# Experts of a token-routed layer: from 96 tiles of 128 rows to 80 pairs of 64-row tiles on the two halves of TensorE's columns

## The reference

```
logits = x @ router_w                      # 2048 tokens, 32 experts
probs = softmax(logits);  topk_w, topk_idx = top_k(probs, 4);  topk_w /= sum(topk_w)
act = silu(x @ w_gate[e]) * (x @ w_up[e])  # 256 -> 192, for each of a token's 4 experts e
routed = sum over e of topk_w * (act @ w_down[e])      # 192 -> 256
shared = silu(x @ sh_gate) * (x @ sh_up) @ sh_down * sigmoid(x @ sh_gate_w)
x = x + tanh(g_ffn[1]) * (routed + shared)
```

## Time and profile before

| | us |
|---|---|
| time, median of 3 runs | 1495.78 |
| lowest and highest of them | 1491.2 and 1495.98 |
| time of the profiled execution | 1492.29 |
| its span, first to last instruction | 1490.6 |

### The profile page before, as it was taken

How to read it: one execution, slowest core, us unless ns; L and a number is a source line. 1 busy time by engine, 2 the same in 40 slices (tenths; PEclk the granted TensorE clock), 3 DMA queues, 4 the chain that set the end, 5 groups by cost and what they waited for, 6 DMA issues and landing times. The chain is left out here.

```text
span 1490.6 us, 24628 instructions
## 1 busy us (share of the span) xinstructions
PE 1290.0 (87%) x8472; PEld 995.4 (67%) x8472; DVE 749.2 (50%) x1642; ACT 673.0 (45%) x1507; POOL 649.1 (44%) x600
## 2 busy tenths in 40 slices
PE   2899862999999999999999199996969899999970
PEld 0555541888888888888888167775636666666640
DVE  2677635444444444455443256664565444444437
ACT  1677731545555455555453065563212155555530
POOL 3222104466666555566664222210112277777740
PEclk9999975999999999999999599997789999999995
DMA  5333343344444444445443465002000155555528
GB/s 156 43 58 58 54 131 130 76 105 106 104 104 106 102 99 99 99 99 103 117 88 36 119 193 190 23 2 71 30 1 1 56 162 159 161 159 162 147 72 282
DMA packets 173340, 151.33 MB, mean 102 GB/s; under 512 B 79414, under 2 KB 141884, under 8 KB 173249
## 3 DMA queue, kind: packets, MB, share of 16 engines
q1 hardware_dynamic: 137152, 93.52, 21.7%
q0 software_dynamic: 33792, 54.57, 18.2%
q10 hardware_dynamic: 2304, 2.10, 0.4%
HBM read 112.37 MB, written 41.94 MB: 104 GB/s over the span
## 5 line engine op out<-in xcount | busy, mean ns | idle before, releaser
L1084 POOL DMA_INDIRECT x_dram<-e_y,rows x128 | 218.4, 1706 | 198.7 <-ACT e_y L1188 174.0
L1117 PE MATMUL bank<-e_xg_hi,e_w_hi 128*128 128x512 f32 x512 | 158.4, 391 | 0.0
L1117 PE MATMUL bank<-e_xg_hi,e_w_lo 128*128 128x512 f32 x512 | 158.0, 390 | 0.0
L1076 POOL DMA_INDIRECT e_xtok<-xn_dram,rows x128 | 125.5, 981 | 74.5 <-issue 38.4
L1117 PE MATMUL bank<-e_xg_lo,e_w_hi 128*128 128x512 f32 x512 | 157.7, 389 | 0.0
L1178 ACT CAST e_hidden_hi<-e_hid 128x512 fp32r<-128x512 f32 x128 | 79.5, 621 | 160.1 <-DVE e_hid L1222 160.1
L1222 DVE TENSOR_TENSOR e_hid<-e_sg,bank 128x512 f32<-128x512 f32 x128 | 88.1, 688 | 125.0 <-PE bank L1117 91.0
L1683 PE MATMUL bank<-e_wt,e_xT 128*128 128x384 f32 x384 | 148.5, 510 | 0.7 <-ACT e_wt L1727 0.6
L1225 DVE TENSOR_TENSOR e_hidden_lo<-e_hid,e_hidden_hi 128x512 fp32r<-128x512 f32 x128 | 88.6, 692 | 88.0 <-ACT e_hidden_hi L1178 88.0
L1659 POOL DMA_INDIRECT ys_dram<-e_yt,tile_dest x96 | 97.0, 1011 | 54.5 <-issue 35.0
L1117 PEld LDWEIGHTS bank<-e_xg_hi,e_w_lo 128*128 128x128 f32 x512 | 96.4, 188 | 20.2
(11 more groups left out here) (264 smaller groups left out, 2547.2 us busy)
## 6 DMA issues: line engine op xcount, KB each, us to landing
e_w<-in_L_ffn_w SPq DMA_DIRECT2D x48, 512.0 KB, 5.0
e_wd<-in_L_down SPq DMA_DIRECT2D x96, 192.0 KB, 2.8
wgu<-in_L_gate_up SPq DMA_DIRECT2D x8, 1536.0 KB, 7.3
c_y<-ys_dram SPq DMA_DIRECT2D x16, 512.0 KB, 8.3
X<-in_x SPq DMA_DIRECT2D x1, 2048.0 KB
b_cT<-in_ctx_t SPq DMA_DIRECT2D x8, 256.0 KB, 6.1
v_dram<-b_vtok SPq DMA_DIRECT2D x16, 128.0 KB, 1.8
b_vs<-v_dram SPq DMA_DIRECT2D x16, 128.0 KB, 3.4
```

The source lines that it names most:

```text
L1076: nc.gpsimd.indirect_dma_start(out=xtok[q][:, :], out_offset=None, in_=xn_dram[:, :], in_offset=bass.IndirectOffsetOnAxis(ap=rows[:, e, q: ...
L1084: nc.gpsimd.indirect_dma_start(out=x_dram[:, :], out_offset=bass.IndirectOffsetOnAxis(ap=rows[:, e, q:q + 1], axis=0), in_=y[q][:, :], in_ ...
L1117: last = nc.tensor.matmul(bank[f % 2][:, :], w[:, k * F0 + f * 128:k * F0 + (f + 1) * 128], x[:, k, h * SLOTS:(h + 1) * SLOTS], start=(w, ...
```

## The change

The tiles become half as high (TT = 64) and are run in pairs (PT = 128 rows). `PAIRS` = 80 pairs replace the 96 tiles. The two tiles of a pair can have different experts. Gathers, scatters, transposes, Silu and the copies of VectorE and ScalarE stay as they were, one for each pair. `up` and `down` become two matmuls in place of each one, with 64 stationary columns each: tile u of the pair goes to half u of the array's columns and of the PSUM partitions, and has its own weights as moving operand. So two sets of weights are needed for a pair: ScalarE copies those of tile 0, VectorE those of tile 1 (new), SyncE loads two sets of down weights, with three buffers for each in place of four. Both `take_weights` now stand last in their loop and run one pair further ahead; in VectorE's loop `take_tokens` stands ahead of `gated`. The routing finds the number of tiles by an add and a shift in place of a comparison with all edges and a sum, and the experts of even and odd tiles in two columns. The diff, cut:

```diff
-TT = 128
+TT, PT = 64, 128
-TILES = -(-((B * S * TOPK + E1 * (TT - 1)) // TT) // 4) * 4
+PAIRS = -(-(B * S * TOPK + E1 * (TT - 1)) // PT)
...
-            count = upto[:, B, :].rearrange("p (e o) -> p e o", o=1).broadcast_to((128, E1, B * S // TT))
-            ch.link(nc.vector.tensor_tensor(over[:, :, :], count, edge[:, :, :], ALU.is_gt))
-            ch.link(nc.vector.tensor_reduce(ntiles[:, :], over[:, :, :], AX_X, ALU.add))
+            ch.link(nc.vector.tensor_scalar(whole[:, :], upto[:, B, :], float(TT - 1), None, ALU.add))
+            ch.link(nc.vector.tensor_scalar(tiled[:, :], whole[:, :], TT.bit_length() - 1, None, ALU.logical_shift_right))
+            ch.link(nc.vector.tensor_copy(ntiles[:, :], tiled[:, :]))
...
-            ch.link(nc.vector.tensor_scalar(done[:, :], ends[:, :], tile_at[:, 0:1], None, ALU.is_le))
-            ch.link(nc.vector.tensor_reduce(te[:, :], done[:, :], AX_X, ALU.add))
+            for u in range(2):
+                last = nc.vector.tensor_scalar(done[:, u, :], ends[:, :], tile_at[:, u:u + 1], None, ALU.is_le)
+            ch.link(last)
+            ch.link(nc.vector.tensor_reduce(te[:, :], done[:, :, :], AX_X, ALU.add))
...
-    NBUF = 4
+    NBUF = 3
...
             def load_down(t):
-                e = sp.value_load(tile_expert[0:1, t:t + 1], min_val=0, max_val=E1 - 1)
-                sp.dma_start(wd[t % NBUF][:, :, :].rearrange("p k n -> p (k n)"),
-                             a["L1_down"][bass.ds(e, 1), :, :].rearrange("o p n -> p (o n)")).then_inc(wd_in[t % NBUF], 16)
+                for u in range(2):
+                    e = sp.value_load(tile_expert[0:1, u, t:t + 1], min_val=0, max_val=E1 - 1)
+                    sp.dma_start(wd[t % NBUF][u][:, :, :].rearrange("p k n -> p (k n)"),
+                                 a["L1_down"][bass.ds(e, 1), :, :].rearrange("o p n -> p (o n)")).then_inc(wd_in[t % NBUF], 16)
...
                 for k in range(KD):
-                    last = nc.tensor.matmul(GU[t % 2][:, 0:2 * F1], xT[t % 2][:, k, :],
-                                            wt[t % NBUF][:, k * 2 * F1:(k + 1) * 2 * F1], start=k == 0, stop=k == KD - 1)
+                    for u in range(2):
+                        last = nc.tensor.matmul(GU[t % 2][half(u), 0:2 * F1], xT[t % 2][:, k, half(u)],
+                                                wt[t % NBUF][u][:, k * 2 * F1:(k + 1) * 2 * F1], start=k == 0, stop=k == KD - 1)
...
                 for m in range(2):
-                    last = nc.tensor.matmul(Y[t % 2][:, 0:D], hidT[t % 2][:, m, :], wd[t % NBUF][:, m, :],
-                                            start=m == 0, stop=m == 1)
+                    for u in range(2):
+                        last = nc.tensor.matmul(Y[t % 2][half(u), 0:D], hidT[t % 2][:, m, half(u)], wd[t % NBUF][u][:, m, :],
+                                                start=m == 0, stop=m == 1)
...
@@ scalar
             gate(0)
+            take_weights(NBUF)
             gate(1)
...
-                if t + NBUF < TILES:
-                    take_weights(t + NBUF)
-                if t + 1 < TILES:
+                if t + 1 < PAIRS:
                     take_hidden(t + 1)
+                if t + NBUF + 1 < PAIRS:
+                    take_weights(t + NBUF + 1)
@@ vector
+            def take_weights(t):
+                e = dve.value_load(tile_expert[0:1, 1, t:t + 1], min_val=0, max_val=E1 - 1)
+                if t >= NBUF:
+                    dve.wait_ge(gu_ps, t - NBUF + 1)
+                nc.vector.tensor_copy(wt[t % NBUF][1][:, :], wgu[:, bass.ds(e, 1), :].rearrange("p o n -> p (o n)")
+                                      ).then_inc(wt1_sb, 1)
...
             take_tokens(0)
             take_tokens(1)
+            for t in range(NBUF):
+                take_weights(t)
             gated(0)
             take_tokens(2)
+            take_weights(NBUF)
             gated(1)
-            for t in range(TILES):
-                if t + 2 < TILES:
+            for t in range(PAIRS):
+                if t + 3 < PAIRS:
+                    take_tokens(t + 3)
+                if t + 2 < PAIRS:
                     gated(t + 2)
-                if t + 3 < TILES:
-                    take_tokens(t + 3)
                 take_result(t)
+                if t + NBUF + 1 < PAIRS:
+                    take_weights(t + NBUF + 1)
```

More of the change, by code:

```diff
@@ L1308, in routing1_phase @@
         value = sb("value", [128, TOPK, B])
-        places = sb("places", [128, TT])
-        tiles = sb("tiles", [128, TILES])
+        places = sb("places", [128, PT])
+        tiles = sb("tiles", [128, PAIRS])
         at_place = [t[:, :, :].rearrange("p b e -> p (b e)").rearrange("p (k n) -> p k n", k=TOPK) for t in choice]
[L1312 to L1318, removed]
+        at_tile = [t[:, :, :].rearrange("p b e -> p (b e)")[:, 0:TOPK * PAIRS].rearrange("p (k n) -> p k n", k=TOPK)
+                   for t in (ex, mine, member, expert)]
+        found, empty = (t[:, :, :].rearrange("p b e -> p (b e)")[:, 0:PAIRS] for t in (before, totals))
+        clipped = sb("clipped", [128, PAIRS], I32)
+        tile_at = sb("tile_at", [128, 2])
+        done = sb("done", [128, 2, E1])
+        te = sb("te", [128, 2])
         (wr_in, w_in, xb_sb, xt_ps, xt0_sb, xt1_sb, l_ps, made, max_sb, ex_sb, sig_sb, mem_sb, cnt_ps, te_sb, te_ps,
@@ L1349, in _ @@
             iota(expert[:, :, :], [[0, B], [1, E1]])
[L1350 to L1353, removed]
+            iota(tile_at[:, :], [[1, 2]], 2)
+            iota(places[:, :], [[1, PT]])
+            iota(tiles[:, :], [[1, PAIRS]])
             iota(value[:, :, :], [[B * S, TOPK], [S, B]], 1, 1)
@@ L1430, in find @@
                 for k in range(TOPK):
-                    last = nc.tensor.matmul(MAP[:, 0:TILES], at_place[b % NMAP][:, k, :], at_tile[b % NMAP][:, k, :],
+                    last = nc.tensor.matmul(MAP[:, 0:PAIRS], at_place[b % NMAP][:, k, :], at_tile[b % NMAP][:, k, :],
                                             start=b == 0 and k == 0, stop=b == B - 1 and k == TOPK - 1)
@@ L1458, in _ @@
             pe.wait_ge(te_sb, 1)
-            nc.tensor.matmul(TE[0:1, 0:128], te[:, :], r.ident[:, :], start=True, stop=True).then_inc(te_ps, 1)
+            for u in range(2):
+                last = nc.tensor.matmul(TE[0:1, u * 128:(u + 1) * 128], te[:, u:u + 1], r.ident[:, :], start=True, stop=True)
+            last.then_inc(te_ps, 1)
             down(1)
@@ L1663, in _ @@
             for v in range(NXT):
-                pool.wait_ge(y_out[v], 16 * (TILES // NXT))
+                pool.wait_ge(y_out[v], 16 * len(range(v, PAIRS, NXT)))
         @block.tensor
@@ L1672, in turn_over @@
                 for k in range(KD):
-                    last = nc.tensor.transpose(XT[t % 2][:, k * TT:(k + 1) * TT], xt[t % NXT][:, k * 128:(k + 1) * 128],
+                    last = nc.tensor.transpose(XT[t % 2][:, k * PT:(k + 1) * PT], xt[t % NXT][:, k * 128:(k + 1) * 128],
                                                r.ident[:, :])
@@ L1691, in turn_hidden @@
                 for m in range(2):
-                    last = nc.tensor.transpose(HT[t % 2][0:FH, m * TT:(m + 1) * TT], hid[t % 2][:, m * FH:(m + 1) * FH],
+                    last = nc.tensor.transpose(HT[t % 2][0:FH, m * PT:(m + 1) * PT], hid[t % 2][:, m * FH:(m + 1) * FH],
                                                r.ident[:, :])
```

75 lines of the change are left out of this document (40 added, 35 removed).

## The result

The changed kernel takes 1462.32 us (median of 4 runs, 1458.5 to 1463.18), the kernel before 1495.3 beside it: ratio 0.9778, 95% interval 0.9759 to 0.9797. That is 33 us less; the forecast was 30.8 less than the 1495.8 known then, to 1465. The profiled execution took 1461.86 with a span of 1460.1, 30.5 under that of before; the sum had -29.5.

The account below looks back on a forecast made before the run. TensorE was taken to bound the experts' stage: 96 tiles at 2.72 us become 80 pairs at 2.89, -29.9, with -0.4 and +0.8 making -29.5. That gave 1462.8 or 1466.3; forecast 1465 us, range 1455 to 1484.

Parts of the forecast that it names:

- the sum: Whole kernel: -29.9 for the experts' stage, -0.4 for routing, +0.8 for the first `up`, together -29.5 us.
- The bound: Experts' stage: TensorE, busy 100 of 100 us there, stays the bound, with a period of 2.89 us per pair.
- Full overlap of the halves: `up` and `down`: half-width matmuls on different columns run side by side, so work stays 2.58 us, plus 0.03.
- The switch: TensorE, once in and out per pair: changing between full and divided array costs 0.28 us, bounds 0.18 to 0.35.
- The four terms: Array change per pair: 0.09 in, 0.04 first weight load, 0.09 out, 0.06 second transpose's load, in us.
- the later starts: `up` and `down` per pair: 0.03 us added because the second half's matmuls start later.
- The stalls: TensorE before `up`: 0.06 us waiting for `xT` and 0.075 of unhidden weight load per tile, both go.
- The new copy: VectorE's 128 x 768 weight copy between SBUF tensors takes 0.57 us per pair, hidden under TensorE.
- Routing and start: Routing chain -0.6 and a small matmul 0.2, net -0.4 us; first `up` +0.8 us, bound 1.5.
- The last pairs drain as before: End of the experts' stage: no change in time for the last pairs.
- The first rival: Experts' stage: GpSimd's DMAs and VectorE's new copy exclude each other, period 3.05 to 3.17, 1478 to 1487 us; chance 0.18.
- Its DMAs still at 1.0: Sign in the experts' stage: GpSimd's DMAs keep 1.0 us; the prediction is wrong if they grow.

Follow-up runs that it names:

- Experiment 4: Changed kernel with `turn_over(t + 3)` moved between `down` and `up`, so full-width transposes split the half-width work once more per pair: 1482.31 us, 0.992 of before.
- experiment 3: Changed kernel with loops of `up` and `down` exchanged, all of tile 0's matmuls before tile 1's: 1465.55 us, 0.9797 of the kernel before.
- experiment 5: Changed kernel with the halves one behind the other and, from the third pair, both tiles' outputs on columns 0 to 63: 1629.25 us, one run.
- the grouping: Changed kernel with two pairs' work between two changes of TensorE's array, plain copy: 1507.41 us, 0.9728 of before; repeated 1505.42 us, 0.9702.
- experiment 1: Kernel before, whole tiles of 128, with VectorE's `take_tokens` ahead of `gated`: 1482.75 us, 0.9911 of before.
- experiment 2: Changed kernel with `gated` back ahead of `take_tokens`: 1462.09 us, 0.9778 of the kernel before.
- the other form: Changed kernel with VectorE's weight copy written as the larger of each value and itself: 1506.89 us, 0.9734 of before; repeated 1507.79 us, 0.971.

## Why the prediction was right

*The bound.* It said that TensorE stays the bound. Experiment 4 shows it for the first chip: 0.30 us more work, 0.30 us more period.

*Full overlap of the halves.* Predicted 0.03 for tile 1 beside tile 0, from a burst of 32 columns. Shown by experiments 3 and 5, whose kernels differ in nothing but the columns: 1.51 against 2.75 for `up`. They ran on different chips, but the record of `up` takes 486 ns in both. The 0.03 wasn't there: the second half's record starts 0.007 behind the first's. What the trace of before couldn't tell, and what I then got wrong in the expectation of experiment 3, is whether the order in the program matters. It hardly does.

*The switch.* Predicted 0.28 (0.18 to 0.35), measured 0.30 by experiment 4, 2 x 0.145 = 0.29 by the grouping, and 0.284 between the periods of experiment 1 and of the kernel after (2.594 and 2.878). The four terms hold too, by the starts in the trace of after: into the half width 0.09 (predicted 0.09), the first load 0.05 (0.04), out 0.10 (0.09), the second transpose 0.04 (0.06). The short neighbour in attention was enough. The full-width work, put at 2.58, is the 2.594 of experiment 1; this 0.014 too little and the 0.03 too much for the later starts leave the 2.89 for 2.88.

*The stalls.* That both go was right, and experiment 1 shows that both had one cause. The text didn't say what this implies: without half tiles the same 0.12 a tile, 12 us, could be had by order alone. In the kernel after, the new order isn't what removes them (experiment 2); the later `down` does.

*The new copy.* 0.57 predicted, 0.56 measured: the slope of the like operations held from 256 to 768 elements. Three of the 80 copies took 0.60 to 0.78.

*Routing and start.* -0.4 predicted; the chain, from the first copy of the counts to the addition that TensorE waits for, fell from 15.77 to 15.16, by the 0.6 predicted. From there to the first transpose 0.86 came back, most of it before the list `tile_rows` was done, where the text had only a small matmul of 0.2. What took it wasn't looked into. The sum of this term was +0.25 and not -0.4. +0.8 was predicted for the first `up`, +1.1 measured, within its bound of 1.5. VectorE's two copies of tokens were done at 1181.53, and 0.60 more went before its first weight copy at 1182.13:

```profile
1180.74 0.79 DVE L1782 COPY e_xT<-bank 128x256 f32<-128x256 f32 x2 [4.31 <-PE bank L1681]
...
1182.13 0.56 DVE L1775 COPY e_wt<-wgu 128x768 f32 x1 [0.60 <-issue]
1182.76 0.32 PEld L1693 LDWEIGHTS bank<-e_wt,e_xT 128*64 128x64 f32 x4 [2.10 <-ACT e_wt L1738]
1182.79 1.55 PE L1693 MATMUL bank<-e_wt,e_xT 128*64 128x384 f32 x4 [1.73 <-DVE e_wt L1775]
```

That is the 0.60 where I had taken 0.2 for reading the register. The copy is what `up` waits for: with the other form, 0.40 longer, `up` starts 3.21 behind the first transpose instead of 2.81.

*The end.* "The last pairs drain as before" was wrong twice, with opposite signs. The last results are copied 1.37 and 1.36 us apart instead of 1.09 and 0.86, as each `turn_hidden` and `down` now costs a round trip of the array, and the last `down` waits 0.28 for its e_wd: +1.0. Then the first load of `combine` starts 6.89 us after the last scatter instead of 9.54: -2.6. All the other kernels with pairs have 6.88 or 6.89 there, and the other whole-tile kernel (experiment 1) has 9.54, so it belongs to the change and not to the execution. Its cause wasn't tried. That the sum of -29.5 came within 1 us of the 30.5 is partly luck: the +1.4 ahead of the chain and the -2.2 at the end (+1.0, -0.6, -2.6), which the text didn't have, nearly cancel.

*The first rival.* Its mechanism is real and its price was far off. Scatters beside the weight copy take up to 1.36 instead of 1.01, but their mean is only 0.09 above. All scatters and all copies from 1200 to 1400 us (least, median, most, in ns):

```profile
L1667 POOL DMA_INDIRECT ys_dram<-e_yt,tile_dest x69: 1012/1014/1361, 1201.2 to 1398.3; - x69
...
L1775 DVE COPY e_wt<-wgu x70: 559/560/783, 1201.0 to 1399.5; 128x768 f32 x70
```

With a scatter of 1.10, a gather of 1.01 and 0.30 of idle time behind each, GpSimd needs 2.71 for a pair, still 0.17 under TensorE. "Its DMAs still at 1.0" is the one mark of the prediction that failed, and the text had named it as a sign that the prediction is wrong; as such it was too strict. It cost nothing: a scatter and a copy that meet do so for only 0.24 us on average, and GpSimd has the 0.17 to give. What matters is which starts first. The 72 operations of GpSimd that start inside a copy take 1.13 in the mean; the 15 in which a copy starts keep their 0.99, and there the copy takes 0.58, at most 0.78. The rival's full blocking, up to 1.0 for VectorE and 0.57 for GpSimd, occurs nowhere. The Trainium skill, SBUF — State Buffer, section "SBUF: two separate sides", says that such a copy keeps GpSimd from writing descriptors, and that a VectorE operation with two SBUF inputs stands only against a GpSimd operation that reads SBUF. By the first half the trace agrees in kind. The operation with two inputs held the scatters longer than the copy did (1.40 against 1.10), and more than the 1.01 of those that it doesn't touch; whether a scatter counts there as a reader of SBUF, by its list of rows, no run here shows.

## What to carry to other kernels

When small groups leave a matmul's stationary side half filled, put two on different column halves: they run together, in whatever order the program has them, and the price is one round trip of the array, 0.29 us here, so do as much divided work as possible between two full-width operations. Before such a rebuild, read the present period for stalls and remove them alone: here an exchange of two calls had 12 of the 33 us. Compare on one chip: a stage that TensorE's work bounds on one was bounded on another by reports of TensorE that came late, with nearly the same ratio to before. And don't name a waiter's releaser by exclusion: look for an engine that waits for only one of the suspects, as ScalarE, which waits for no transfer, did here.

## What the runs showed of the hardware that wasn't expected

- Program order between the two column halves costs 0.05 us in 2.9; the second half's matmuls start while the first half's stand unfinished ahead of them (0.013 us behind the first record).
- Two chips took 3.6 and 3.7% longer for the kernel before. In the traces from them the first `up` still starts between 1180 and 1186 us, as on the first chip (1180 to 1188). For the kernel after 49 of the 51 us lie between the first and the last `up`, 276.5 us instead of 227.2. There `down` reports to VectorE up to 2.1 us behind its last record (25 times in 200 us); on the first chip it takes at most 0.03.
- From the last scatter to the first load of what was scattered: 9.54 us with 96 whole tiles, 6.89 with 80 pairs.
- A maximum of two equal SBUF operands takes 0.96 us for 768 float32 values where the copy takes 0.56, and beside it a scatter took up to 1.74 us instead of 1.01.
- An indirect DMA that GpSimd starts during a 0.56 us copy of VectorE takes 1.13 us in the mean; one that it started before the copy keeps its 0.99.
